# Attention on one core: the inverse of the softmax sums is taken, stored and spread earlier in each unit, and GpSimd divides one pair of sums later

## The reference

```python
xn = layernorm(x)
q, k, v = bitnet_linear(xn, wq, sq), bitnet_linear(xn, wk, sk), bitnet_linear(xn, wv, sv)   # 32 heads of 32; 8 key/value heads
scores = einsum('bhqd,bhkd->bhqk', q, k) / sqrt(32)
attn = softmax(scores, axis=-1)
out = einsum('bhqk,bhkd->bhqd', attn, v)
x + bitnet_linear(out, wo, so) + dot(silu(dot(xn, G)) * dot(xn, U), Dn)     # G, U, Dn dequantised from integers
```

## Time and profile before

| | |
|---|---|
| median of 3 executions | 2636.39 us (2632.84 to 2636.93) |
| the profiled execution: its time | 2635.6 us |
| the profiled execution: its span | 2633.6 us |
| mean granted TensorE clock | 0.962 of full speed |
| PE, DVE, ACT, POOL busy | 92%, 69%, 59%, 37% of the span |
| attention, from the second unit to the end | 376 to 1290 us |

### The profile page before, as it was taken

One profiled execution on the slowest core, in us unless ns is written; L12 is line 12 of the kernel. 1 busy time (PEld: TensorE's weight loads), 2 busy tenths in 40 slices (PEclk: granted clock), 3 DMA queues, 4 the chain that ended last, 5 costly groups with the idle time before them and its releaser, 6 DMA issues.

```text
span 2633.6 us, 33630 instructions
## 1 busy us (share of the span) xinstructions
PE 2421.2 (92%) x12408; PEld 968.9 (37%) x12408; DVE 1828.4 (69%) x2362; ACT 1559.0 (59%) x1988; POOL 983.0 (37%) x545
## 2 busy tenths in 40 slices
PE   2499899989999999999689999999999999999998
PEld 1344322222222222222234444444444444444444
DVE  6756687766676767666154777777777777777777
ACT  3633267766676777667512666666666566666664
POOL 1000058788787888879600112122000112122000
PEclk9799889999999999999789999999999999999999
DMA  5100045544545455455412111112111311012211
GB/s 165 64 4 33 22 79 81 87 68 74 75 75 83 69 80 72 74 79 73 102 68 92 33 32 49 32 42 98 45 41 64 128 32 49 32 47 101 101 41 64
DMA packets 173711, 174.65 MB, mean 66 GB/s; under 512 B 87587, under 2 KB 119203, under 8 KB 173559
## 3 DMA queue, kind: packets, MB, share of 16 engines
q1 hardware_dynamic: 111286, 150.62, 18.2%
q0 software_dynamic: 62272, 22.03, 10.9%
HBM read 160.08 MB, written 65.45 MB: 86 GB/s over the span
## 4 chain that ended last, share of the span: by engine, by line
PE 54%; POOL 8%; issue 6%; DVE 1%; ACT 1%; DMA 1%; SPq 0%; DVEq 0%; POOLq 0%; ACTq 0%
PE ps L1309 29%; PE ps L1325 15%; POOL zone L504 6%; PE ps L1289 4%; PE ps L1212 2%; PE ps L1201 1%; POOL dequantised L525 1%; PE ps L1224 1%; PE ps L1185 1%; POOL zone L513 1%; PE ps L1341 0%; DMA zone<-in_L_attn_o_weight_dram 0%; ACT zone L657 0%; DVE zone L1098 0%; POOL zone L508 0%
## 5 line engine op out<-in xcount | busy, mean ns | idle before, releaser
L934 DVE TENSOR_REDUCE zone<-ps 128x1 f32<-128x512 f32 x1024 | 639.6, 683 | 271.5 <-PE ps L1185 271.3
L657 ACT ACTIVATE zone<-ps,sm 128x512 f32<-128x512 f32 x1024 | 631.6, 690 | 267.2 <-PE ps L1201 170.5
L1309 PE MATMUL ps<-xT,zone 128*128 128x512 f16 x3584 | 774.6, 379 | 3.6 <-DVE zone L1098 2.8
L504 POOL TENSOR_TENSOR zone<-zone 128x1024 f32<-128x1024 f32 x256 | 649.7, 2689 | 69.9 <-ACT zone L657 41.0
L1075 DVE TENSOR_SCALAR ps<-ps,zone_c 128x1024 f32<-128x1024 f32 x392 | 506.8, 1293 | 161.1 <-PE ps L1309 159.2
L725 ACT ACTIVATE ps<-ps,zone_c 128x1024 f32<-128x1024 f32 x392 | 426.8, 1089 | 261.1 <-PE ps L1309 259.3
L1309 PEld LDWEIGHTS ps<-xT,zone 128*128 128x128 f16 x3584 | 350.1, 98 | 427.4 <-DVE zone L1098 4.2
L1201 PE MATMUL ps<-zone 98*128 98x512 f16 x1024 | 392.9, 387 | 55.7 <-ACT zone L657 55.7
L1185 PE MATMUL ps<-zone 96*128 96x512 f16 x1024 | 405.2, 397 | 11.3 <-DMA zone<-zone 10.5
L1325 PE MATMUL ps<-zone 128*128 128x512 f16 x1792 | 387.1, 379 | 0.0
L1086 DVE TENSOR_SCALAR ps<-ps,zone_c 128x1024 f32<-128x1024 f32 x216 | 279.3, 1293 | 93.0 <-PE ps L1325 92.9
(11 more groups left out here) (127 smaller groups left out, 1292.6 us busy)
## 6 DMA issues: line engine op xcount, KB each, us to landing
zone<-dequantised SPq DMA_DIRECT2D x84, 512.0 KB, 3.6
dequantised<-zero_points SPq DMA_DIRECT2D x84, 256.0 KB, 4.1
zone<-zone SPq DMA_DIRECT2D x384, 32.0 KB, 2.3
zone<-_attn_hidden_states_dram SPq DMA_DIRECT2D x16, 512.0 KB, 6.8
zone<-inverse_sums SPq DMA_DIRECT2D x128, 64.0 KB, 2.5
attention<-zone SPq DMA_DIRECT2D x32, 256.0 KB, 2.0
xT<-attention SPq DMA_DIRECT2D x4, 2048.0 KB, 12.0
dequantised<-in_L_ffn_gate_w_dram POOLq DMA_DIRECT2D x28, 256.0 KB, 6.4
```

The source lines that it names most:

```text
L504: nc.gpsimd.tensor_tensor(duo[n % 3], prob[:, e % 8, :], prob[:, (e + 2) % 8, :], add).then_inc(s["sum_ok"], 1)
L657: A(prob[:, e % 8, m % 2 * 512:(m % 2 + 1) * 512], ps[:, 3 + m % 3, :], ACT.Exp, scale=gam[:, 0:1]).then_inc(s["exp_ok"], 1)
L934: V.tensor_reduce(mxs[:, u % 2, half, i % 16:i % 16 + 1], ps[:, (2 * i + half) % 3, :], AX, amax).then_inc(s["max_ok"], 1)
L1309: last = MM(ps[:, 4 * s2 + 2 * m + c, :], ring[:, buf, m * H + g * P:m * H + (g + 1) * P], xT[:, hf, part, g, c * 512:(c + 1) * 512], star ...
```

## The change

Four once-per-unit pieces stand at other steps; no instruction is added or taken away and none has another size.

```diff
@@ SyncE
                 if k == 8 and u + 1 < UNITS:
                     load_m(u + 1)
+                if k == 11 and u:
+                    store_inverse(u - 1)
                 if k == 13 and u:
-                    store_inverse(u - 1)
-                if k == 15 and u:
                     spread_inverse(u - 1)
                 if k == 14 and u + 3 < UNITS:
                     sp.wait_ge(s["st_pe"], 32 * u + 32)
@@ GpSimd
             for u in range(UNITS):
-                if u >= 2:
-                    divide(u - 2)
                 for j in range(4):
                     for hp in range(2):
                         add_pair(u, j, hp)
                         n = duo_of(u, j, hp)
                         if n % 3 == 2 and n // 3 < TILES:
                             add_weights(n // 3)
+                    if u >= 2 and j == 0:
+                        divide(u - 2)
                     if u >= 2 and j == 2:
                         tail_of(u - 2)
@@ ScalarE
-                if k == 7 and u >= 2:
+                if k == 10 and u >= 2:
                     head_of(u - 2)
@@ VectorE
-                if k == 12 and u:
+                if k == 10 and u:
                     invert(u - 1)
```

## The result

The changed kernel takes 2542.27 us as the median of 4 executions (2541.42 to 2542.98); the kernel before took 2635.86 us in the same comparison. The ratio is 0.9647, with a 95% interval from 0.963 to 0.9663: faster by 3.5%. The profiled execution took 2542.98 us, 92.6 us less than the one of before.

A forecast was written before the change was run, and what follows sets the result against it. In attention, POOL's wait for the late spread inverse was taken to hold units above PE's pace. -94.0 us for 28 units and +2.8 for small terms gave -91.2, from about 2636 to 2545 us; range 2540 to 2568.

The forecast's parts named there:

- The bound: Attention, 28 units: without POOL's wait for the inverse, each runs at PE's 26.42 us instead of 29.78, -94.0 us.
- The small terms: POOL's group with the division (0 to 0.12 us a unit) and ACT's head_of (0 to 0.21); 0.1 taken, +2.8 us.
- The chain from SP's queue to POOL: Spreading queued behind loads on SP makes POOL's division wait 4.95 us a unit, delaying adds, then PE.
- why the inverse is late is in SP's queue: SP in unit 1: store issued at 394.44, spreading only at 405.65, behind a preset and fifteen loads; landing near 410.
- The margin of SP's new wait: SP's list: waiting for the store's landing ahead of the loads leaves 1.2 us before queries could start; cost nothing.
- POOL as the bound: Rival, chance 0.09: POOL, 94% full, can't fill its gaps; a unit takes 27.27 us, time 2566.
- remaining wait for PE's sums: POOL at L1224: once the wait for the inverse is gone, it waits for PE's sums, about 50 us in all.
- The slower rival: Chance 0.02: store landings 8.0 us beyond the median delay SP's loads until PE loses everything gained; at 11 us, 2676.
- the slack of 3.4 us: Keys in unit 1: they land at 407.7 and PE first needs them at 411.11, a second cover for late loads.
- The rival of the late loads: Chance 0.05: slow store landings on SP bring queries 3.8 us late, keys 0.4 us too late; 11 us back, 2556.
- 3.36 us a unit: Attention's 28 units before the change: 29.78 - 26.42 us, time that is not PE's own work, 94.0 us in all.
- is part of them: PE's granted clock of 0.96 instead of 1.00 over the 28 units makes up part of the 3.36 us a unit.

The follow-up runs named there:

- both halves alone: Kernel before with only SyncE's and VectorE's edits (reciprocal, store, spreading earlier): 2541.10 us; with only GpSimd's and ScalarE's (division, head_of later): 2542.77 us.
- one-line kernel: Kernel before with only the spreading of the inverse moved ahead of the query loads (k = 15 to k = 14): 2546.56 us.
- four added products: Changed kernel with four extra 128x512 products on POOL in each of 28 units, on a scratch buffer, behind every group: 2590.07 us.
- two added products: Changed kernel with two extra 128x512 products on POOL in each of 28 units, on a scratch buffer, behind groups 1 and 3: 2542.46 us.

## Why the prediction was right, point by point

*The bound.* That a unit without POOL's wait runs at PE's 26.42 us is shown: 26.44 measured over 28 units, and the same pace in both halves alone. The sum was -94.0 us for it; 93.5 was measured over the 28 units.

*The small terms.* I took 0.1 us a unit (2.8 us) for a group on POOL that is 0.1 us too long and for `head_of`. Measured 0.015 us a unit, 0.4 us in all. Both were at their lower bound: PE waits for neither. That is most of the difference between 2545 and 2542.3.

*The chain from SP's queue to POOL.* Its links are all in the profile, but "why the inverse is late is in SP's queue" was half of the cause. The runs of the halves show two sufficient cures: SP's part lands the inverse ahead of the old asking, POOL's part asks behind the old landing. My own numbers held this already (landing near 410, asking at 410.7 us, and the landing in the trace is at 409.1), but I had added the two edits up as one.

*The margin of SP's new wait.* Reckoned 1.2 us, measured 1.25. The store lands after 1.5 us as a median and 5.5 at most, all 32 of the changed kernel:

```profile
DMA to landing us min/median/max: 1.4/1.5/5.5
```

The prediction let the median decide, 1.6 us, and that was the wrong summary of the rows. Among the 29 stores of the units 1 to 29 in the kernel before, ten were issued 2.7 to 3.6 us behind one of POOL's transfers of weights, which take 6.4 us to land, and landed after 2.5 to 4.3 us; the fifteen that were issued 5.0 to 7.5 us behind one landed after 1.4 to 1.7, and four close behind one took 1.4 to 4.7. In the one-line kernel the store stands 1.1 or 3.4 us behind one in 20 units of 29, and its median is 2.8. This agrees with the rule of the Trainium skill ("DMA: Bandwidth & Descriptors", section "Queues, rings and completion order") that an increment lands behind all earlier writes of its DMA engine, but not in every store: of the ten in the changed kernel that are issued 0.5 or 0.6 us behind a transfer of weights seven land after 1.4 or 1.5 us and three after 5.1 to 5.5. No run tells the rule from plain sharing of the DMA engines. That the median of the changed kernel came out at 1.5 was in part luck: the store's new place was not chosen for it.

*POOL as the bound.* It was given a chance of 0.09, and it did not happen: POOL needs 26.44 - 63.3 / 28 = 24.2 us a unit, and it becomes the bound between two and four added products. My forecast of its remaining wait for PE's sums (about 50 us) was 63.3.

*The slower rival.* The place was right, the size was not. I put the point from which it decides at 8.0 us beyond the median landing. The loads four steps later are 6.55 us late, which with the margin of 1.2 stands for 7.8 us, and that kernel is already 19 us slower than before: the slack of 3.4 us was reckoned with median landings (two steps later lost 17.7 us inside it), and the clock falls behind the longer stalls. The rival of the late loads was too cheap for the same reasons: it priced loads that are 3.8 us late at 11 us, and the run in which they are 2.85 us late lost 17.7. In the changed kernel itself none of this happens.

*The accuracy of "3.36 us a unit".* It is right as a sum, and it isn't idle time alone: PE was busy for 775.99 / 28 = 27.7 us a unit before and for 26.4 after, so 1.3 of the 3.3 us were longer work. The traces tell how much of that is the clock. In the unit from 459.42 to 489.75 of the kernel before PE stands for ACT, and then the same eight matmuls of L1212 take 1.93 us that take 1.07 a few us later:

```profile
470.93 0.39 PE L1201 MATMUL ps<-zone 98*128 98x512 f16 x1 [1.85 <-ACT zone L657]
...
472.00 1.93 PE L1212 MATMUL ps<-zone 128*32 128x512 f32 x8
...
477.27 1.07 PE L1212 MATMUL ps<-zone 128*32 128x512 f32 x8
```

In the windows the granted clock (the column behind POOL's) is 0.50 behind the stall, the lower of its two levels (1.2 GHz). From 475.42 to 479.42 it is 1.00 again, with PE busy all the time.

```profile
472.42:474.42 2.00, 2.00 (x12) 0.20 (x8) 0.00 (x0) 0.49 (x1) 2.00 (x2) 0.50 1.11 86
```

Of the 28 units 12 have a clock of 1.00 over their length, and PE is busy for 26.8 us in each as a mean; the other 16 have 0.90 to 0.95, and it is busy for 28.4. By these means some 16 x 1.67 = 27 of the 37.4 us by which PE's busy time fell are the clock's (an estimate), and some 11 are not. With four added products the clock stayed at 1.00 and PE's busy time still rose, to 715.16 / 739.88 of 28.15 us, 27.2. One reading of that, which no run tests, is that matmuls that stand apart overlap less in the record: back to back, a row of L1201 or L1185 lasts 0.38 us and the next starts after 0.22. So the prediction's words that the clock "is part of them" hold, and the whole came back because the stalls went.

## What to carry to other kernels

A wait on a transfer has two ends. Before building both cures, write down when the data lands and when it is asked for: here moving either one was enough, and moving the spreading alone, by one line, gave 89 of 93 us. An engine at 37% of the span can be at 91% of its stage and have two free microseconds a unit, and not the 16 that 37% suggests; read its waits inside the stage, which told its slack within 0.1 us a unit when work was added. Take a queue's slack from its slowest landings, not from medians, and look at what was issued just ahead of the slow ones. Price a stall of PE with the clock that may fall behind it.

## What the runs showed of the hardware

A product on POOL of a 128x512 buffer with itself, written in place, takes 1.00 us from start to start, while the product of two different buffers, written into one of them, takes 1.22 to 1.24. In the kernel with two added products, where L516 is the added one and L509 the division:

```profile
596.39 1.46 POOL L509 TENSOR_TENSOR zone<-zone 128x512 f32<-128x512 f32 x1
597.62 2.55 POOL L505 TENSOR_TENSOR zone<-zone 128x1024 f32<-128x1024 f32 x1
...
603.07 1.86 POOL L516 TENSOR_TENSOR zone<-zone 128x512 f32<-128x512 f32 x1
604.07 5.58 POOL L505 TENSOR_TENSOR zone<-zone 128x1024 f32<-128x1024 f32 x2
```

597.62 - 596.39 = 1.23 and 604.07 - 603.07 = 1.00. The durations in the rows, 1.46 and 1.86 us, are longer than the spacing of back-to-back instructions, so on POOL the spacing is what to count. Whether it is the shared input or the place of the buffer that saves the 0.23 us was not tried.

Two facts from above belong here too. In the one-line kernel, units 1 to 29, the small store landed after 1.4 to 1.7 us when the last transfer of weights had been issued 6.6 to 8.2 us earlier, and after 3.6 to 4.3 us when it had been issued 1.1 us earlier. And a stall of PE can cost more than its length: PE idle from 469.1 to 470.9 us was followed by a granted clock of 0.50, and in the kernel before PE's busy time was 28.4 us as a mean in units with a clock below 1.00 and 26.8 in the others.
